# Attention scores of four heads at a time from 64 rows each, keys spread over four blocks instead of eight

## The reference, cut to what matters

```python
q = q.reshape(b, t, H, Dh).transpose(0, 2, 1, 3)            # H = 16 heads, Dh = 16 features
scores = jnp.einsum('bhtd,bhsd->bhts', q, k) / jnp.sqrt(jnp.float32(Dh))
scores = jnp.where(causal, scores, -jnp.inf)                # or an additive mask, or none
probs = jax.nn.softmax(scores, axis=-1)
out = jnp.einsum('bhts,bhsd->bhtd', probs, v)
```

## Time and profile before

| | |
|---|---|
| median of three runs | 8310.44 us |
| span of the profiled execution | 8333.2 us; the profile gives no time outside the span, and it lies within the three runs |
| TensorE busy | 6721.0 us (81%) |
| VectorE busy | 3959.2 us (48%) |
| ScalarE busy | 1842.1 us (22%) |
| GpSimd busy | 1376.6 us (17%) |
| the five attention stages | 5101 to 5794, 6530 to 6795 and 7100 to 7705 us of the span, 1563 us together |

### The profile page before, as it was taken

The page is one execution under the profiler, slowest core; times in us unless marked ns, Lnnn a source line. Parts: engine busy times, 40 slices in busy tenths (PEclk is TensorE's granted clock), DMA queues, the critical chain, the costliest instruction groups (busy, mean ns, idle before and its releaser), DMA issues. The chain is left out here.

```text
span 8333.2 us, 92849 instructions
## 1 busy us (share of the span) xinstructions
PE 6721.0 (81%) x34116; PEld 4705.7 (56%) x34116; DVE 3959.2 (48%) x8807; ACT 1842.1 (22%) x2726; POOL 1376.6 (17%) x1101
## 2 busy tenths in 40 slices
PE   5889888888888888898599998876476766778698
PEld 3666665666666566666456665554243543555454
DVE  7454455654445565444300003545487344554444
ACT  2222122222222222221121211222211233223111
POOL 2221122222212222221200001312000100222100
PEclk8776677676666767766799999877655777778899
DMA  0000000000000000000000000000000000000000
GB/s 26 1 1 1 1 1 1 1 1 1 1 1 1 1 1 1 1 1 14 35 11 21 21 11 6 0 25 13 2 1 8 20 4 4 3 17 6 4 17 23
DMA packets 13607, 64.63 MB, mean 8 GB/s; under 512 B 1168, under 2 KB 5648, under 8 KB 11152
## 3 DMA queue, kind: packets, MB, share of 16 engines
q1 hardware_dynamic: 13200, 59.09, 2.0%
HBM read 56.99 MB, written 2.10 MB: 7 GB/s over the span
## 5 line engine op out<-in xcount | busy, mean ns | idle before, releaser
L806 PE MATMUL psum<-arena,weights 32*32 32x64 f32 x8192 | 860.4, 287 | 0.0
L773 PE MATMUL psum<-arena 128*128 128x256 f32 x2048 | 596.8, 443 | 319.3 <-DVE arena L979 312.6
L806 PEld LDWEIGHTS psum<-arena,weights 32*32 32x32 f32 x8192 | 763.5, 152 | 5.8
L1219 PE MATMUL psum<-arena 128*128 128x512 f32 x1600 | 711.7, 599 | 59.5 <-DVE Y L1283 35.8
L773 PEld LDWEIGHTS psum<-arena 128*128 128x128 f32 x2048 | 448.3, 224 | 526.1 <-issue 349.5
L796 PEld LDWEIGHTS psum<-arena 32*32 32x32 f32 (+2 forms) x6144 | 591.0, 157 | 256.6 <-issue 253.9
L796 PE MATMUL psum<-arena 32*32 32x64 f32 (+2 forms) x6144 | 670.3, 293 | 0.0
L1231 PE MATMUL psum<-arena 128*128 128x256 f32 x2624 | 583.0, 380 | 4.1 <-DVE arena L1324 4.1
L1300 DVE SCALAR_TENSOR_TENSOR Y<-psum,arena,Y 128x256 f32<-128x256 f32 x416 | 172.5, 478 | 849.0 <-PE psum L1231 849.0
L1231 PEld LDWEIGHTS psum<-arena 128*128 128x128 f32 x2624 | 499.1, 190 | 111.7 <-issue 43.5
L144 POOL TENSOR_TENSOR arena<-arena,eps 128x4 f32<-128x4 f32 (+2 forms) x76 | 15.1, 199 | 3221.9 <-DVE arena L139 3221.9
(11 more groups left out here) (418 smaller groups left out, 10541.0 us busy)
## 6 DMA issues: line engine op xcount, KB each, us to landing
arena<-in_experts_L_ffn SPq DMA_DIRECT2D x8, 2052.0 KB, 8.2
arena<-in_ctxT SPq DMA_DIRECT2D x16, 512.0 KB, 3.5
arena<-in_experts_L_ffn SPq DMA_DIRECT2D x18, 384.0 KB, 3.0
weights<-in_w_L_ffn SPq DMA_DIRECT2D x1, 3072.0 KB, 9.8
weights<-in_w_L_attn SPq DMA_DIRECT2D x1, 3024.5 KB, 13.1
weights<-in_w_L_ffn SPq DMA_DIRECT2D x1, 2753.0 KB, 12.8
weights<-in_w_L_relu SPq DMA_DIRECT2D x1, 2436.0 KB, 9.4
X<-in_x SPq DMA_DIRECT2D x1, 2048.0 KB, 8.3
```

Of the source, the lines that this page charges most:

```text
L773: mm = nc.tensor.matmul(ps[:, 2 + 2 * hh + m // 2, (m % 2) * 2 * P:(m % 2 + 1) * 2 * P], kz[:, p % 2, hh, m, :], kq[:, p % 2, m, :, :], st ...
L806: mm = nc.tensor.matmul(ps[rows, 4 + h, m * DK:(m + 1) * DK], Tt[rows, h * M + m, :], rhs, start=True, stop=True)
L1219: mm = nc.tensor.matmul(ps[:, bank, :], W[s][name][:, c, f * P:(f + 1) * P], xT[:, g, c, :], start=(c == 0), stop=(c == C - 1))
```

## The change

Head h of a chunk is now in block h mod 4 (`HQ` = 4). The mask is 128 by 4, the spread keys are 4 blocks of 128 columns (half of the elements), and each block holds two heads: one on its partitions in 0 to 63, the other in 64 to 127. The first score matmul takes partitions 0 to 63 of queries and keys and gives heads 0 to 3 into the first bank; the second takes partitions 64 to 127 and gives heads 4 to 7 into the second. Both still stream 512 columns; the count of matmuls, the waits and the order are as before.

```diff
+HQ = HH // 2
-    km = A(2, HH, P)
+    km = A(2, HQ, P)
                 keys = kT[:, c, u * P:(u + 1) * P]
-                pool.tensor_tensor(km[:, j % 2, :, :], bc(keys, 1, HH), bc(w.heads, 2, P), ALU.mult
+                pool.tensor_tensor(km[:, j % 2, :, :], bc(keys, 1, HQ), bc(w.heads, 2, P), ALU.mult
                                    ).then_inc(keys_spread, 1)
             def recalled_keys(g, u):
-                pool.tensor_tensor(km[:, u % 2, :, :], bc(keys, 1, HH), bc(w.heads, 2, P), ALU.mult
+                pool.tensor_tensor(km[:, u % 2, :, :], bc(keys, 1, HQ), bc(w.heads, 2, P), ALU.mult
                     for b in range(2):
-                        mm = nc.tensor.matmul(out[:, b * 4:b * 4 + 4, :], qT[:, c, u * P:(u + 1) * P],
-                                              km[:, at % 2, b * 4:b * 4 + 4, :], start=True, stop=True)
+                        rows = slice(b * HQ * DH, (b + 1) * HQ * DH)
+                        mm = nc.tensor.matmul(out[:, b * HQ:(b + 1) * HQ, :], qT[rows, c, u * P:(u + 1) * P],
+                                              km[rows, at % 2, :, :], start=True, stop=True)
 def heads_mask():
-    return (np.arange(P)[:, None] // DH == np.arange(HH)[None, :]).astype(np.float32)
+    return (np.arange(P)[:, None] // DH % HQ == np.arange(HQ)[None, :]).astype(np.float32)
```

## The result

The changed kernel takes 8383.72 us, the median of six runs (8355.91 to 8416.82), against 8312.32 us for the kernel before (six runs, 8294.9 to 8350.9). The ratio is 1.0077, with a 95% interval of 1.0042 to 1.0111: slower, where 60 us less were forecast.

What follows compares the result with a forecast made beforehand. It took the five attention stages (1563 of 8333.2 us) to be bound by a path through TensorE, VectorE and ScalarE, with half the score groups on it. 36 + 8 + 20 + 8 - 12 = 60 us less gave 8250 us, range 8185 to 8350.

Steps and rivals of the forecast that it cites:

- the clock: TensorE in the five stages: mean granted clock falls by 0.01, costing 12 us; ends 0 and 0.05 (61 us).
- rival 2: Clock falls behind TensorE's waits for an exponential, as halved scores may not bring it back: 8406 us at 0.66; chance 0.15.
- The price of the clock: Five stages: a fall of 0.01 in the mean clock over 1563 us costs 12 us.
- The sum without its clock term: Gains in the five stages from TensorE's scores and GpSimd's spread, 36 + 8 + 20 + 8, 72 us.
- GpSimd's side: Shorter key spread: 20 us from VectorE's undisturbed subtraction and 8 us at the start of turns, 28 us saved.
- Side by side against in turn: Two score halves on TensorE: 0.86 us a group if side by side, 1.72 if in turn; 0.86 taken.
- Rivals 3 and 4: Score halves overlap by half (8276 us, chance 0.13), or don't overlap at all (8316 us, chance 0.12).
- Changes of shape: TensorE's array changes shape around each score group: two changes cost 0.4 us a group, ends 0 and 0.6.
- TensorE's part: Shorter scores: 80 groups on the path at 0.45 us, 36 us, plus 8 us for first scores of a turn.
- cap unit 5: ScalarE's copy is late next after shorter scores in a masked stage, limiting unit 5's gain to 1.3 us.
- The decision point: Five stages: falling clock makes the kernel slower by over 1% from a fall of 0.13, 0.80 to 0.67.
- The 0.22: Whole kernel: chance of being slower by over 1%, 83 us.

Runs made afterwards that it cites:

- e4: Changed kernel with each score group issued twice, on half rows, so streaming time is that of the kernel before: 8338.01 us, ratio 1.0010 to before.
- e3: Kernel before with each score matmul streaming 256 columns instead of 512 from all 128 rows, half the scores left out: 8369.2 us, ratio 1.0033.
- e10: Kernel before with float32 filler matmuls of 512 columns put into TensorE's waits, results overwritten; a repeat run: 8205.08 us, ratio 0.9851.
- e9: Changed kernel with float32 filler matmuls of 512 columns put into TensorE's waits, results overwritten; a repeat run: 8145.15 us, ratio 0.9778 to before.
- e2: Changed kernel with keys still spread over four blocks, but both score matmuls from all 128 rows (two heads added in each score): 8289.26 us, ratio 0.9938.
- e8: Changed kernel with filler matmuls in TensorE's waits, but both score matmuls from all 128 rows (two heads added in each score): 8191.3 us, ratio 0.9839.
- e1: Changed kernel with half-row score matmuls kept, but keys and mask again over eight blocks as before: 8396.23 us, ratio 1.0062 to before.

## Why the prediction was wrong

**The step that failed** is the clock: "I take 0.01; ends 0, and 0.05 (61 us)". The clock fell by 0.13, and that is rival 2, which had a chance of 0.15; its place, its cause (the scores are the long streams behind the waits) and its sign were as written. The earlier trace rows had been read as saying that small tiles don't bring the clock back. e4 shows that half rows do (0.82) when the streaming time is there, and e3 that full rows fall short without it (0.69). In these runs the clock went with how long the scores stream: 0.81 in full, 0.69 and 0.68 when halved, 0.82 when given back. The prediction counted what a fall costs and not how near to it the kernel stood: at 7.32 us a unit there is no wait left in which TensorE idles, and the clock stayed at 1.2 GHz for over 29 us.

**The price of the clock was about right.** 12 us for 0.01 had been worked out. Between e10 and the kernel before the clock differs by 0.14 and the stages by 145 us, and between e9 and the change by 0.24 and 238 us: 10 us for 0.01, in the same code but for fillers. At 10 us (an estimate, worked out from those two pairs) the fall of 0.13 cost about 130 us, and the change without it would have gained 130 - 62 = 68 us in the stages. The sum without its clock term was 72. The kept-busy pair, e9 against e10, gives 31 us at a clock lower by 0.035, by the same rate 66. That 12 came so near is in part luck: the prediction names two groups of values a pair, and its sum of 4.7 us has only one (1.75 us); with both it would be 6.4 us in 12, and the price about 17 us for 0.01.

**The other terms**, corrected for the differing clocks by the same 10 us for 0.01 (so estimates, and rough where the correction is larger than what is left):

- GpSimd's side, 20 + 8 = 28 us forecast: e2 45 us less at 0.015 more clock, so 30; e8 against e10 12 less at 0.012 lower, so 24; the change against e1 2 less at 0.016 lower, so 18. About right. The subtraction's mean is 1226 ns in the change, at the undisturbed time (1277 in e2 and e8, where the scores still take as long as before), and the spread takes 1053 ns against 1.04 us taken from the row of line 696.
- Side by side against in turn: right, though the nearest row was one of column tiles. By the strict order of matmuls that the prediction set against it, a group would take 1.28 us; with changes of shape and all it took 1.17, and where no copy is late 1.06 (5292.15 to 5293.21 in e9). Rivals 3 and 4 fall.
- Changes of shape, 0.4 us a group: about right. e4 streams as long as the kernel before, and its unit in the last stage takes 4.75 us (7630.87 to 7635.62) against 4.29 in e10: 0.15 more ahead of the scores, 0.20 behind them and 0.11 in the values, 0.46 in all. e9's unit, at 4.00 us with 0.86 less streamed, has 0.57, but there the values wait for ScalarE's copy, so 0.11 may be that wait. e4 against e2 is 49 us, 41 with the clock corrected: 0.26 us for each of 160 units, or 0.51 if 80 count.
- TensorE's part, 36 + 8 = 44 us: e9 against e8 is 19 less at 0.023 lower clock, so 42 by the correction, which is larger than the difference itself. That this meets 44 does not show the term right. A group gives 0.29 us in the last stage and 0.06 in the rotary one, not 0.45, since ScalarE's copy is late next. The prediction had that copy cap unit 5 at 1.3 us, read from a turn in which TensorE was at the low clock; at 2.4 GHz next to nothing is left under the cap. 80 groups at 0.29 would be 23 us. How many lie on the path was not tested.

**The decision point** of rival 2 was put at a clock of 0.67, where the kernel would be 1% slower. At 0.68 it was 0.8% slower. The chance given to "within 1%" held the outcome, but the range ended at 8350 us, half way down rival 2, and the forecast had the wrong sign. The 0.22 was the chance of a loss of over 1%; what the chance of a loss of any size was, the prediction never said.

## What to carry to other kernels

Before TensorE's work is shortened, see what keeps its clock up: where short matmuls stand beside a few long ones, and the granted clock is already between the two levels, halving the long ones can cost more than it saves. Keep the waits filled first, and shorten then: the same change is a loss by itself and a gain with the clock kept up, and the change with fillers beats both kernels (0.9778 of the kernel before; the kernel before with the same fillers reaches 0.9851). Price the clock as its own term, from a run at another clock of the same stages, and ask how far the kernel stands from the fall. And look again at what is late next when the clock is up: here it was ScalarE's copy, which in the rotary stage took nearly all that the shorter scores give.

## What the runs showed of the hardware

- Two float32 matmuls from rows 0 to 63 and 64 to 127, into two PSUM banks, run side by side: from four records of 512 columns to the values behind them it is 1.17 us at 2.4 GHz (1.06 where no copy is late), changes of shape included, against 1.72.
- TensorE can be busy without a gap and be held at 1.2 GHz: 7.32 us a unit with turnings, halved scores and 17-column values, for 29.41 us on end. The same work also ran at 2.4 GHz in the same execution (3.98 us a unit). More streaming (e4) brought the clock of the five stages from 0.68 to 0.82 and shortened TensorE's busy time there (1324.7 to 1256.8 us).
- VectorE's subtraction of two operands in the arena stood still beside GpSimd's spread for up to 1.3 us (2.52 instead of 1.22 us); with the spread out of its way its mean is 1226 ns. The Trainium skill says so (SBUF — State Buffer, section "SBUF: two separate sides": of a VectorE operation with two SBUF inputs and a GpSimd one that reads SBUF, whichever starts first has the shared port pair for its whole instruction, and the other blocks), and this trace agrees: GpSimd had started 0.46 us before.
